# A graph network kernel: four of every 32 gathered edge columns fetched by one-hot products, and node products scaled out of PSUM

## The chip, the cores and the metric

The kernel runs on one core of one Trainium2 chip. The metric is the device time of one execution in microseconds (us). The core has five engines: TensorE (PE, with its weight loads shown apart as PEld), VectorE (DVE), ScalarE (ACT), GpSimd (POOL) and SyncE (SP, which issues plain DMAs). They meet through semaphores.

## The reference

Four layers run over one graph with 6250 nodes, 64 features and 200000 edges sorted by destination. Each layer reads a table of node rows by the source of every edge and sums per destination. The first layer does that three times.

```python
for i in range(3):                                   # layer 0, weights W, b
    mv = proj(mobius_matvec(W[i], h, c), c)
    h = proj(mobius_add(mv, proj(expmap0(b[i][None, :], c), c), c), c)
    ht = logmap0(h, c)
    msgs = edge_weight[:, None] * ht[edge_col]       # a row of the table per edge
    agg = jax.ops.segment_sum(msgs, edge_row, num_segments=N_NODES)
    h = proj(expmap0(jax.nn.relu(logmap0(proj(expmap0(agg, c), c), c)), c), c)
...
h = jnp.maximum(_layernorm(x, axis=-1), 0.0)         # ahead of layers 1, 2 and 3
x = x + _L1_gnn_ref(h, edge_attr_16, ...)            # attention
x = x + _L2_gnn_ref(h, edge_index, edge_attr_8, ...) # relu of [x[src], x[dst], attr] @ W1 + b1, then @ W2 + b2
x = x + _L3_gnn_ref(h, src, dst, ...)                # attention
```

## The kernel before

**Preparation.** In the first 2.1 ms the edges are put into buckets by destination tile. There are T = 49 tiles of 128 nodes. Each bucket is padded to groups of 256 edges, and the groups lie in DRAM as `packed`. There are NG = 832 groups. A group is two columns of 128 edges, one edge a partition.

**Six passes.** PLAN lists three convolution passes ("gcn"), an attention pass, an "mlp" pass and an attention pass. Each pass runs over all 832 groups in ITER = 52 iterations of BODY = 16 groups, that is 32 columns. Before each pass, node work on DVE, PE and ACT makes the table Y (128 partitions x 52 rows x 65 values). SP stores it to DRAM as `table`. Node (tile t, partition p) is row p*52 + t of the table.

**An iteration of a convolution pass.** SP loads 32 columns of row numbers from `SRC` into `idx`, in two halves. POOL issues one indirect DMA for each column (`gathers`, L412), which fetches 128 rows of the table into `G`. `G` has 32 columns, so POOL may refill a column once PE has summed that column's group of the iteration before (`agg_ready`). DVE makes two weighted one-hot matrices for each group (`weighted_one_hot`, L676): 1 times the edge's weight where the destination fits. PE multiplies them with the gathered rows (`sums`, L1346), two f32 products of 128x64 that the trace shows as four passes. DVE adds the result from PSUM to the accumulator of the group's tile (`add_up`, L797). The order on DVE is written out: one-hot of group g, then `add_up` of group g-1. One-hots have a ring of 8 groups. `ps_a` has two banks, so the sums of g wait for `add_up` of g-2.

**Start of an iteration on DVE.** `tiles_of` (L659) loads 24 numbers into registers, which say to which tile each group belongs. In the first convolution pass, `unpack` stands ahead of that for all but the last three iterations. It takes 32 columns out of `packed` for an iteration that comes three later (16 DVE instructions and two that end them).

**Node products.** `node_product` goes through the 52 tiles in 13 steps of 4. PE transposes U, ACT copies the transpose to SBUF, PE multiplies it with weights, and ACT copies the result out of PSUM (`copied`). Ahead of attention, DVE then multiplies Y and er by the reciprocal deviation `small["a"]`. Ahead of the mlp pass, U is scaled and put through a ReLU before the product starts.

## Time and profile before

| what | us |
|---|---|
| median of three runs | 15381.07 |
| lowest and highest of them | 15380.45 to 15383.63 |
| the profiled execution, as timed | 15402.48 |
| its span, first to last instruction | 15400.7 |
| preparation, up to the first gathers | about 2140 |
| convolution passes with their node work | about 2140 to 8660 |
| attention, mlp, attention | about 8660 to 15400 |

The profile divides the span by engine and by line. A row of the timeline has a start, a duration, an engine, a line, the operation, what is written and read, and in brackets how long the engine had been idle and what ended the idle time.

### The profile page before, as it was taken

The numbers are of one execution on the slowest core, as the hardware profiler recorded it, in microseconds if no ns is written. First come the engines' busy times: TensorE is split into PE (matmuls) and PEld (weight loads), VectorE is DVE, ScalarE is ACT, GpSimd is POOL, SyncE is SP. The second block draws the span as 40 slices with busy tenths as digits, with TensorE's granted clock in tenths as the row PEclk, the third lists the DMA queues.
The fourth block names the chain that finished last, engine by engine and source line by source line (L and its number), as shares of the span: only waits on it lengthen the run. The fifth ranks groups of instructions, "written<-read, shape, count | busy, mean of one in ns | idle before, by whom it ended". The sixth has DMA issues, their size and how long they took to land.

```text
span 15400.7 us, 287262 instructions
## 1 busy us (share of the span) xinstructions
PE 7779.5 (51%) x57314; PEld 6635.2 (43%) x57315; DVE 8734.1 (57%) x40002; ACT 3613.7 (23%) x12048; POOL 11064.0 (72%) x11556
## 2 busy tenths in 40 slices
PE   0000004444444444444444588888556565788887
PEld 0000003333333333333333577777444444677777
DVE  7860014444443333433333688888777777788888
ACT  1000000000000000000000366666322222566666
POOL 4777777777767777677777677777577777677776
PEclk9985555555555555555555555555555555555555
DMA  2111112222111111111111111111111111111111
GB/s 97 25 25 26 26 36 41 41 39 41 37 28 27 27 27 27 28 27 27 27 27 27 27 26 26 26 26 26 23 28 28 28 28 28 27 28 27 27 27 28
DMA packets 519941, 468.03 MB, mean 30 GB/s; under 512 B 301517, under 2 KB 326733, under 8 KB 518222
## 3 DMA queue, kind: packets, MB, share of 16 engines
q0 software_dynamic: 369664, 358.70, 14.1%
q1 hardware_dynamic: 149454, 102.38, 2.4%
q14 instruction: 797, 6.53, 0.1%
q8 instruction: 26, 0.43, 0.0%
HBM read 389.15 MB, written 65.20 MB: 30 GB/s over the span
## 4 chain that ended last, share of the span: by engine, by line
DVE 31%; issue 24%; PE 20%; POOL 12%; DVEq 7%; DMA 5%; ACT 1%; POOLq 0%; SPq 0%; ACTq 0%
PE bank L1346 17%; POOL packed L393 9%; DVE OH L676 7%; DMA G<-table,idx 5%; DVE r_gm L709 3%; POOL G L412 3%; DVEq L659 2%; DVE OHB L687 2%; DVE ACC L797 2%; DVE ACC L803 1%; DVE e_arg L754 1%; DVE r_a L712 1%; DVE e_w L749 1%; DVE r_a L716 1%; DVEq L797 1%
## 5 line engine op out<-in xcount | busy, mean ns | idle before, releaser
L412 POOL DMA_INDIRECT G<-table,idx x9984 | 9535.3, 955 | 3614.3 <-issue 2125.6
L1346 PE MATMUL bank<-G,OH 128*128 128x64 f32 x9984 | 2704.1, 428 | 4840.5 <-DVE OH L676 3941.4
L1346 PEld LDWEIGHTS bank<-G,OH 128*128 128x128 f32 x9984 | 2310.9, 322 | 5233.7 <-DVE OH L676 4254.6
L797 DVE TENSOR_TENSOR ACC<-ACC,bank 128x64 f32 x2496 | 552.0, 221 | 3404.0 <-PE bank L1346 3401.8
L393 POOL DMA_INDIRECT packed<-Y,slab_pos x1568 | 1528.5, 975 | 670.3 <-issue 494.7
L676 DVE TENSOR_SCALAR OH<-const,DL,W 128x128 f32<-128x128 f32 x4992 | 1755.8, 400 | 409.2 <-PE bank L1346 269.9
L1346 PE MATMUL bank<-ZR,OH 128*128 128x65 f32 x6656 | 1765.3, 419 | 0.0
L1346 PEld LDWEIGHTS bank<-ZR,OH 128*128 128x128 f32 x6656 | 1623.8, 334 | 0.2
L1408 PE MATMUL bank<-ER,OHT 128*128 x9984 | 995.6, 174 | 712.5 <-DVE negm_lo L738 542.1
L1180 ACT ACTIVATE OHT<-bank 128x256 f32<-128x256 f32 x91 | 35.6, 391 | 5473.0 <-PE bank L1324 5471.9
L1408 PEld LDWEIGHTS bank<-ER,OHT 128*128 128x128 bf16 x9984 | 781.9, 104 | 1005.8 <-issue 877.7
L1396 PE MATMUL bank<-const,V 128*128 128x128 f32 x3328 | 1114.9, 439 | 22.8 <-ACT V L1241 22.6
L687 DVE TENSOR_TENSOR OHB<-iota_b,DLw 128x256 bf16<-128x256 bf16 x2496 | 1054.2, 422 | 38.7 <-ACT V L1241 31.6
L1385 PE MATMUL bank<-ident_b,OHB 128*128 128x128 bf16 x4992 | 1009.1, 305 | 48.8 <-DVE OHB L687 48.8
L1216 ACT ACTIVATE OHT<-bank,const 128x256 bf16<-128x256 f32 x1664 | 788.0, 474 | 527.3 <-PE bank L1385 490.7
L1234 ACT ACTIVATE OH<-OHB,const 128x256 f32<-128x256 bf16 x1664 | 824.9, 496 | 40.5 <-DVE OHB L687 23.3
L1216 ACT ACTIVATE OHT<-bank 128x256 bf16<-128x256 f32 x832 | 319.5, 384 | 1660.1 <-PE bank L1438 1660.1
L709 DVE TENSOR_REDUCE r_gm<-bank 128x1 f32<-128x256 f32 x1664 | 694.3, 417 | 10.5 <-PE bank L1396 10.5
L467 DVE TENSOR_SCALAR W<-Z 128x16 f32 (+1 forms) x104 | 20.4, 196 | 1190.8 <-DMA Z<-packed 1154.9
L1385 PEld LDWEIGHTS bank<-ident_b,OHB 128*128 128x128 bf16 x4992 | 615.9, 135 | 157.9 <-DVE OHB L687 49.8
L1444 PE MATMUL bank<-WE,E8T 128*128 128x128 bf16 x832 | 239.2, 287 | 829.5 <-DVE OH L769 683.4
L1241 ACT ACTIVATE V<-OHB,EL 128x128 f32<-128x128 bf16 x1664 | 576.7, 393 | 227.7 <-DVE EL L695 211.0
(273 smaller groups left out, 14164.1 us busy)
## 6 DMA issues: line engine op xcount, KB each, us to landing
G<-table,idx POOLq DMA_INDIRECT x9984
packed<-Y SPq DMA_DIRECT2D x42, 640.0 KB, 17.7
Z<-packed SPq DMA_DIRECT2D x104, 256.0 KB, 2.7
Y<-in_payload SPq DMA_DIRECT2D x98, 256.0 KB
packed<-Y,slab_pos POOLq DMA_INDIRECT x1568
table<-Y SPq DMA_DIRECT2D x6, 1690.0 KB, 5.5
idx<-SRC SPq DMA_DIRECT2D x624, 8.0 KB
X<-in_x SPq DMA_DIRECT2D x1, 1568.0 KB, 8.3
```

The lines of the kernel that those rows point to most:

```text
L393: pool.indirect_dma_start(out=packed_rows, out_offset=bass.IndirectOffsetOnAxis(ap=slab_pos[:, h, c:c + 1], axis=0), in_=slab[:, h, c, :], ...
L412: pool.indirect_dma_start(out=G[:, 2 * q + c, :], out_offset=None, in_=table, in_offset=bass.IndirectOffsetOnAxis(ap=idx[:, h, j:j + 1], a ...
L676: o = v.tensor_scalar(OH[:, q, c, :], iota, DL[:, at], W[:, at], ALU.is_equal, ALU.mult)
L687: v.tensor_tensor(OHB[:, q, :, :], iota_b[:, :].unsqueeze(1).to_broadcast([P, 2, P]), DLw[:, 2 * u:2 * u + 2].unsqueeze(2).to_broadcast([P ...
L709: v.tensor_reduce(sr["gm"][:, r:r + 1], ps_x[r % 2][:, 0:GE], AX.X, ALU.max).then_inc(a_done, 1)
L797: v.tensor_tensor(acc, acc, ps_a[r % 2][:, 0:D], ALU.add).then_inc(acc_done, 1)
L1216: return a.activation(OHT[:, r, :], ps_m[r % 2][:, 0:GE], ACT.Identity, scale=scale, bias=bias)
L1234: a.activation(OH[:, q, :, :], OHB[:, q, :, :], ACT.Identity, scale=-1.0, bias=ones[:, 0:1])
L1346: o = pe.matmul(ps_a[r % 2][:, 0:w], OH[:, q, c, :], parts[c], start=c == 0, stop=c == 1)
L1385: o = pe.matmul(ps_m[r % 2][:, c * P:(c + 1) * P], OHB[:, q, c, :], ident_b[:, :], start=True, stop=True)
L1396: o = pe.transpose(ps_x[r % 2][:, c * P:(c + 1) * P], V[:, r % 4, c, :], ident)
L1408: pe.matmul(e[:, c:c + 1], one, ER3[:, bass.ds(t, 1), k], start=k == 0, stop=k == 2)
```

## The change

**Four columns from a table on chip.** In a convolution pass POOL gathers only the first 28 of 32 columns of each iteration (`fetched(n)` is 14 groups of 16). Groups 14 and 15 get their rows otherwise. Before the pass, `three_parts` splits the table Y into three bf16 parts that add up to it (`table_parts`, 49 tiles x 3 x 64, in the memory of U and Z). In an iteration, DVE copies the four columns of row numbers (`choose`, at group 10 of the iteration before). PE spreads them over all partitions with four f32 products against the identity (`spread`, at group 12). ACT subtracts 52 times the partition number while it copies to bf16 (`codes`). At the start of the iteration DVE compares this 128x512 code with each tile number 0 to 48, one instruction a tile (`tile_hots`). PE multiplies each result's four 128x128 matrices with the 128x192 table parts of that tile (`rows_from_table`), and sums over the tiles in two banks. At group 4 DVE adds the three parts out of PSUM into `G` (`take_rows`). The compared matrices have 8 slots, so DVE is at most 8 tiles ahead of PE.

**Node products.** In products 3 to 6 DVE, not ACT, takes the result out of PSUM and multiplies by `small["a"]` or adds on the way (`each_step`). ACT puts the ReLU on the transposes. The whole-table multiplications and the ReLU on DVE go. The product starts as soon as U is centred, ahead of the squares. DVE's part of the eviction comes after its reduction and the square root.

```diff
@@ gathers, indices: fetched(n) of 16 groups
+        def fetched(n):
+            return BODY - ON_CHIP // 2 if PLAN[n][0] == GCN else BODY
-                        for q in range(BODY // 2 * h, BODY // 2 * (h + 1)):
+                        for q in range(BODY // 2 * h, min(BODY // 2 * (h + 1), fetched(n))):
@@ DVE
+                def choose(i):
+                    need(v, code_spread, i + n * (ITER + 1))
+                    at = i * (2 * BODY) + (2 * BODY - ON_CHIP)
+                    move(chosen[:, :], SRC[:, ds(at, ON_CHIP)]).then_inc(chosen_ready, 1)
+                def tile_hots(i):
+                    j = i * T + n * ITER * T
+                    v.wait_ge(code_ready, i + (n * (ITER + 1) + 1))
+                    for tile in range(T):
+                        need(v, tile_used, j + max(tile - SLOTS + 1, 0))
+                        v.tensor_scalar(tile_hot(tile), code, float(tile), None, ALU.is_equal).then_inc(tile_ready, 1)
+                def take_rows(i):
+                    v.wait_ge(tile_used, i * T + (n * ITER * T + T))
+                    need(v, agg_ready, i * BODY + gb)
+                    for k in range(ON_CHIP // 2):
+                        q = BODY - ON_CHIP // 2 + k
+                        got = ps_rows[k][:, 0:6 * D].rearrange("p (s k c) -> p s c k", s=2, k=3)
+                        v.tensor_reduce(G[:, 2 * q:2 * q + 2, 0:D], got, AX.X, ALU.add).then_inc(taken[k], 1)
...
+                    if live(0) and u == 0:
+                        tile_hots(i)
+                    if live(0) and u == 4:
+                        take_rows(i)
+                    if live(0) and u == 10:
+                        choose(i + 1)
@@ PE
+                def spread(i):
+                    pe.wait_ge(chosen_ready, i + (n * (ITER + 1) + 1))
+                    need(pe, code_ready, i + n * (ITER + 1))
+                    for c in range(ON_CHIP):
+                        o = pe.matmul(ps_code[:, c * P:(c + 1) * P], chosen[:, c:c + 1].to_broadcast([P, P]), ident,
+                                      start=True, stop=True)
+                    o.then_inc(code_spread, 1)
+                def rows_from_table(i):
+                    for k in range(ON_CHIP // 2):
+                        need(pe, taken[k], i + n * ITER)
+                    for tile in range(T):
+                        pe.wait_ge(tile_ready, i * T + (n * ITER * T + tile + 1))
+                        for c in range(ON_CHIP):
+                            o = pe.matmul(ps_rows[c // 2][:, c % 2 * 3 * D:(c % 2 + 1) * 3 * D],
+                                          tile_hot(tile)[:, c * P:(c + 1) * P],
+                                          table_parts[:, tile, :, :].rearrange("p k c -> p (k c)"),
+                                          start=tile == 0 and c % 2 == 0, stop=tile == T - 1 and c % 2 == 1)
+                        o.then_inc(tile_used, 1)
...
+                        if u == 0:
+                            rows_from_table(i)
+                        if u == 12:
+                            spread(i + 1)
@@ before each convolution pass
+                three_parts([table_parts[:, :, k, :] for k in range(3)], Y[:, :, 0:D], sums_of)
@@ node products, attention
+                def take(at, got):
+                    own.count(v.tensor_tensor(small["er"][:, at], got[:, :, ROW], small["a"][:, at], ALU.mult))
+                    return scaled(Y[:, at, :], got[:, :, 0:ROW], at)
                 centre_and_start()
-                tt(Y[:, :, :], Y[:, :, :], small["a"][:, :].unsqueeze(2).to_broadcast([P, TP, ROW]), ALU.mult)
-                tt(nodes(small["er"]), nodes(small["er"]), nodes(small["a"]), ALU.mult)
+                each_step(take)
```

The order of instructions on DVE, at the start of an iteration of the first convolution pass, was this before (OH are the one-hots of a group, ACC the accumulator, sched the tile numbers):

```order
L1036 SCALAR_TENSOR_TENSOR SRC<-itmp 128x16
L659 ISA
L659 TENSOR_LOAD sched
L661 ISA x2
L80 REGISTER_ALU
L676 ISA
L676 TENSOR_SCALAR OH<-const,DL,W 128x128
L676 ISA
L676 TENSOR_SCALAR OH<-const,DL,W 128x128
```

In the changed kernel the same place on DVE begins so (OHT and V hold the compared matrices, OHB the code), and 46 more such comparisons follow:

```order
L1120 SCALAR_TENSOR_TENSOR SRC<-itmp 128x16
L703 ISA
L703 TENSOR_LOAD sched
L705 ISA x2
L755 REGISTER_ALU
L83 REGISTER_ALU
L758 TENSOR_SCALAR OHT<-OHB 128x512
L758 TENSOR_SCALAR V<-OHB 128x512
L758 TENSOR_SCALAR OHT<-OHB 128x512
```

The 49 comparisons stand between the register load and the first one-hots of the iteration, so also ahead of the last `add_up` of the iteration before.

On PE, an iteration began before with a wait and the sums of one group after another:

```order
L276 UNCONDITIONAL_BRANCH
L276 ISA
L1350 ISA
L80 REGISTER_ALU
L1346 MATMUL bank5<-G,OH 128x64 x2
L1356 REGISTER_ALU
L1346 MATMUL bank6<-G,OH 128x64 x2
```

Now 49 such blocks of four products stand ahead of the first sums (UZ holds the table parts; three of the blocks are shown):

```order
L1456 REGISTER_ALU
L1458 MATMUL bank2<-UZ,OHT 128x192 x2
L1458 MATMUL bank3<-UZ,OHT 128x192 x2
L1456 REGISTER_ALU
L1458 MATMUL bank2<-UZ,V 128x192 x2
L1458 MATMUL bank3<-UZ,V 128x192 x2
L1456 REGISTER_ALU
L1458 MATMUL bank2<-UZ,OHT 128x192 x2
L1458 MATMUL bank3<-UZ,OHT 128x192 x2
```

No sums of the iteration can start before the last of these 196 products has been issued.

## Rows read from the trace of the kernel before

**Rows 1.** The page: busy time by engine, and the granted TensorE clock in 40 slices.
```profile
PE 7779.5 (51%) x57314; PEld 6635.2 (43%) x57315; DVE 8734.1 (57%) x40002; ACT 3613.7 (23%) x12048; POOL 11064.0 (72%) x11556
...
PEclk9985555555555555555555555555555555555555
```

**Rows 2.** Groups by line in the second convolution pass, 4372 to 6452 us.
```profile
L412 POOL DMA_INDIRECT G<-table,idx x1663 | 1573.5, 946 | 562.3 <-issue 290.9 <-PE bank L1346 215.8 <-DMA idx<-SRC 55.5
L1346 PE MATMUL bank<-G,OH 128*128 128x64 f32 x3320 | 903.9, 428 | 1213.3 <-DVE OH L676 946.4 <-DMA G<-table,idx 144.4 <-issue 117.1
```

**Rows 3.** Timeline, DVE between two iterations: first pass (2628), second pass (5293).
```profile
2628.51 0.22 DVE L797 TENSOR_TENSOR ACC<-ACC,bank 128x64 f32 x1 [1.54 <-PE bank L1346]
...
2635.81 0.60 DVE L676 TENSOR_SCALAR OH<-const,DL,W 128x128 f32<-128x128 f32 x2 [2.25 <-issue]
...
5293.57 0.22 DVE L797 TENSOR_TENSOR ACC<-ACC,bank 128x64 f32 x1 [1.62 <-PE bank L1346]
5296.37 0.64 DVE L676 TENSOR_SCALAR OH<-const,DL,W 128x128 f32<-128x128 f32 x2 [2.58 <-PE bank L1346]
```

**Rows 4.** Timeline after an unpack, when gathered rows lie ready and DVE and PE catch up.
```profile
2636.68 1.96 PE L1346 MATMUL bank<-G,OH 128*128 128x64 f32 x8 [5.83 <-DVE ACC L797]
...
2637.94 0.22 DVE L797 TENSOR_TENSOR ACC<-ACC,bank 128x64 f32 x1 [0.88 <-PE bank L1346]
...
2638.80 0.22 DVE L797 TENSOR_TENSOR ACC<-ACC,bank 128x64 f32 x1
...
2640.16 0.22 DVE L797 TENSOR_TENSOR ACC<-ACC,bank 128x64 f32 x1 [0.50 <-PE bank L1346]
...
2641.16 0.22 DVE L797 TENSOR_TENSOR ACC<-ACC,bank 128x64 f32 x1
```

**Rows 5.** Timeline in the mlp pass: a bf16 instruction on DVE, six bf16 products on PE.
```profile
11503.18 0.19 DVE L467 TENSOR_SCALAR E8S<-V 128x128 bf16<-128x128 bf16 x1
...
11503.28 0.30 DVE L777 SCALAR_TENSOR_TENSOR OH<-OH 128x128 f32<-128x128 f32 x1
...
11503.60 0.50 PE L1458 MATMUL bank<-OH,OHB 128*128 128x65 bf16 x6
```

**Rows 6.** Timeline, PE in a node product: its first passes, and passes 5 us later.
```profile
4320.32 2.08 PE L1324 MATMUL bank<-const,ACC 128*128 128x128 f32 x8 [0.62 <-DVE n_res L644]
...
4325.46 0.61 PE L1324 MATMUL bank<-const,ACC 128*128 128x128 f32 x4
```

**Rows 7.** Stretches: length, busy time (instructions) of PE, PEld, DVE, ACT, POOL, PE clock, DMA.
```profile
4324.40:4334.00 9.60, 9.42 (x84) 9.22 (x83) 9.53 (x3) 9.38 (x42) 0.00 (x0) 1.00 0.00 1
4335.00:4338.00 3.00, 0.00 (x0) 0.00 (x0) 2.50 (x1) 1.69 (x4) 0.00 (x0) 1.00 0.00 0
...
11028.50:11031.70 3.20, 2.38 (x32) 1.76 (x32) 3.13 (x16) 1.11 (x5) 2.29 (x4) 0.97 0.14 23
11032.00:11038.00 6.00, 5.54 (x64) 4.19 (x63) 5.86 (x32) 2.00 (x9) 4.47 (x6) 0.50 0.18 28
```

**Rows 8.** Timeline in the preparation: an indirect DMA issued beside a long DVE instruction.
```profile
978.44 3.62 DVE L451 TENSOR_TENSOR U<-X,n_a 128x3328 f32<-128x3328 f32 x1
979.03 3.87 POOL L393 DMA_INDIRECT packed<-Y,slab_pos  x1 [0.30 <-issue]
```

**Rows 9.** Groups by line and shape, whole span: DVE reduces 256 values out of PSUM.
```profile
L709 DVE TENSOR_REDUCE r_gm<-bank 128x1 f32<-128x256 f32 x1664 | 694.3, 417 | 10.5 <-PE bank L1396 10.5
```

**Rows 10.** Timeline, DVE: the last node product, and a split of a node tensor into bf16 parts.
```profile
13165.51 3.62 DVE L451 TENSOR_TENSOR Z<-U 128x3328 f32<-128x3328 f32 x1
...
13171.10 0.15 DVE L644 COPY n_res<-n_r 128x1 f32<-128x1 f32 x1
...
13185.90 3.68 DVE L451 TENSOR_TENSOR Y<-Y,n_a 128x3380 f32<-128x3380 f32 x1 [9.15 <-ACT Y L1204]
...
11003.75 1.90 DVE L1093 CAST U<-Z 128x3328 bf16<-128x3328 f32 x1
11005.68 3.62 DVE L451 TENSOR_TENSOR Z<-Z,U 128x3328 f32<-128x3328 f32 x1
```

More of the change, by code:

```diff
@@ L51 @@
 AHEAD = 3
+ON_CHIP = 4
+SLOTS = 8
 STEPS_N = TP // 4
@@ L483, in _ @@
             own.count(v.memset(sched[:, :], 0))
+            own.count(v.memset(SRC[:, 2 * NG:], 0))
             own.count(v.memset(rank, 0.0))
@@ L926, in run_pass, with three_parts @@
                 own.wait()
+            def three_parts(parts, what, rest):
+                own.wait()
+                own.count(v.tensor_copy(parts[0], what))
+                tt(rest, what, parts[0], ALU.subtract)
+                own.wait()
+                own.count(v.tensor_copy(parts[1], rest))
+                tt(parts[2], rest, parts[1], ALU.subtract)
             v.wait_ge(sched_loaded, 16)
```

126 lines of the change are left out of this document (82 added, 44 removed).

## The prediction

> **What bounds the kernel now.** I read the page first: POOL is busy 72% of the span, more than any other engine, and the TensorE clock stands at 0.5, that is 1.2 GHz, from the fourth slice on [rows 1]. Then the groups by line in the second convolution pass: 1663 gathers fill 1573.5 + 562.3 us, so one starts every 1.28 us with the pass's start in it, and PE is idle for more time than it is busy [rows 2]. Inside an iteration the step is steadier: 0.95 us and a gap of 0.30, 1.25 us, so 32 columns take 40.1 us. Over 52 iterations that is 2085 us, which is the length of the pass. A convolution pass is bound by POOL's gathers; DVE and PE wait for them. The question is what PE and DVE need for an iteration once they have more to do.
>
> **What is removed.** Four gathers of 1.25 us in each of 156 iterations: 5.0 us an iteration, 780 us in all, if nothing else then needs more than 35.1 us.
>
> **What is added on the path of DVE and PE.** The stretch stands in one piece at the start of an iteration, and the work around it is serial: DVE cannot begin it before `add_up` of group 14, and PE cannot sum group 0 before it is over. So I add up one turn, from `add_up` of group 14 to the next one.
>
> - Start of the iteration on DVE: from one `add_up` to the next instruction 5296.37 - 5293.57 = 2.8 us [rows 3], the register load. POOL covered it before; nothing covers it now, since PE has only group 15 left. The first comparison and its hand-over to PE: 0.5 us, estimated from the 0.3 us that an instruction of that size should take (next but one).
> - The 196 products on PE. Six bf16 products of 64 or 65 columns take 0.50 us [rows 5]; the last one's 0.24 off, that is a step of 0.053 us for 64 columns at 1.2 GHz, with the weight loads hidden. For 192 columns: 0.159 us, 31.2 us for 196. The clock decides. In a node product PE worked without a pause from 4320.32, the f32 steps were 0.213 us (eight passes in 2.08, the first of them a little longer), and from 4324.4 the clock is 1.00 (2.4 GHz) and four passes take 0.61 us, a step of 0.111 [rows 6, 7]: half, and 5 ns. The stretch is denser than that product, so I take the same 4.1 us at 1.2 GHz (26 products), and 170 at 0.083 us: 18.2 us.
> - The 49 comparisons on DVE run beside it. A bf16 instruction of 128 values takes 0.19 us and the next starts 0.10 us after it [rows 5]. 384 more values at four a cycle of 0.96 GHz are 0.10 us: one each 0.20 us, 9.8 us, behind PE's 0.33 us a tile. Covered. At one value a cycle it would be 0.60 us each and 29.4 us, the bound then.
> - The sums of groups 0 to 14. Four passes end 1.1 us after their start (eight take 1.96) [rows 4]. After that DVE and PE go hand in hand, as where they catch up: `add_up` at 2637.94, 2638.80, 2640.16, 2641.16, so two groups in 2.22 and 2.36 us, 2.29 in the mean [rows 4]. 1.1 + 7 x 2.29 = 17.1 us.
> - `take_rows` at group 4: two reductions of 384 values; 256 take 0.417 us [rows 9], so 0.55 each and about 0.5 from start to start: 1.0 us on DVE's path.
> - `spread` at group 12: four f32 products of 128 columns, eight passes of 0.213 us, 1.7 us, less the 0.2 us for which PE pauses at each group there: 1.5 us. ACT's copy and `choose` (0.1 us) are done while groups 13 to 15 are summed.
> - A credit: the clock stays up some 3.5 us after dense work (still 1.00 up to 4338 though PE is not busy from 4335; at 11028.5, with PE busy for 74% of the time, it held for 3.2 us and was 0.50 after that) [rows 7]. Passes at 0.111 take 0.41 us less for a group, and their drain 0.15 less, so 0.56 us for each pair, of which one group's passes lie on the turn. Two pairs: -1.1 us.
> - Hand-over to `add_up`: 0.2 us.
>
> The sum is 2.8 + 0.5 + 18.2 + 17.1 + 1.0 + 1.5 - 1.1 + 0.2 = 40.2 us, against 40.1 before. POOL's 35.1 us lie below it, so they go off the path: the 5 us that the gathers lose are handed to PE and DVE nearly to the last tenth. For 156 iterations: +0.14 x 156 = +22 us.
>
> **The first pass pays more.** There DVE also unpacks: from `add_up` to the next one-hot 2635.81 - 2628.51 = 7.3 us [rows 3], 4.5 more than elsewhere. Before, POOL went on gathering meanwhile and the catching up was free. Now it lies on the turn, 49 times: +220 us.
>
> **Node work.** `three_parts` ahead of each convolution pass: 1.9 + 3.6 + 1.9 + 3.6 = 11 us [rows 10]. Part of it lies beside the table's store, the index load and the first gather's landing, which DVE waited for before; I take 5 us each, +15 (bounds 0 and 33). For attention, 24.1 us went from the centred U to the end of the product with 3.7 us of scaling (13165.5 to 13189.6) [rows 10]. Now the product starts 5.6 us earlier, stops after two steps until DVE has reduced (about 10 us later), and then needs 11 steps at 1.7 us cold or 0.9 warm, some 12.5 us: 2 us less, twice. Product 4 loses a scaling of 3.6 us and a ReLU of 1.9, and squares and reduction (3.6 each) now lie beside it; of these 12.7 us I count all. Product 5 overlaps two of its three whole-table instructions, 7 us. Together -24 us (bounds -40 and +10).
>
> **Sum.** +22 + 220 + 15 - 24 = +233 us on the profiled execution's own 15402.5: 15635. That execution is 21.4 us above the median, so the forecast for a median is 15614; call it 15610.
>
> **Bounds.** The unknowns are the clock and how tightly DVE and PE go hand in hand. Low end: PE stays at 2.4 GHz all through. Then a group's passes end in 0.65 us, a pair takes 0.56 less, 1.73, and spreading 0.8: 2.8 + 0.5 + 18.2 + 0.65 + 12.1 + 1.0 + 0.8 + 0.2 = 36.3 us. High end: the rise comes at 6 us instead of 4.1 (+1.0), and waits on 49 semaphores cost PE 0.03 each (+1.2): 42.4.
> The Trainium skill ("TensorE: Matmul & The Clock Gate", "Back-to-back issue gap") gives a real stream of load and product pairs 81 ns at 128 columns and 131 at 512, warm, so about 90 ns at 192 by interpolation, an estimate from that page; the stretch would be 1.2 us longer by it, and the forecast some 190 us higher. The rows have no warm bf16 stream to hold against it; the cold one steps at exactly its columns.
>
> **Rivals.**
> - Faster: the turn is shorter than I add up. The break-even is 156 x (turn - 40.06) + 220 + 15 - 24 = 0, a turn of 38.7 us. For it: the clock holds in the sums, or DVE, which has finished its last comparisons while PE still has eight tiles to go, gains more than I gave. Against: at 11031.7 the clock fell after 74% busy [rows 7], and at 2.4 GHz a group's passes would fill at most 0.6 of 0.87 us, 70%. At the low end, 36.3 us: 104 x -3.8 + 49 x 0.7 - 3 x 3.8 - 9 = -381 us, 15000. Milder: a turn of 38, 15270.
> - The clock does not rise in the stretch: 31.2 us for it and no credit, a turn of 54.3 us, +2430 us, 17810. Against: it rose within 4.1 us in the node product, and the mlp pass with its bf16 products reached 0.97 too [rows 6, 7].
> - The comparison runs at one value a cycle: 29.4 us, a turn of 51.4, +1980 us, 17360.
> - The comparisons keep POOL out. An indirect DMA that began beside a 3.6 us DVE instruction took 3.87 us instead of 0.96 [rows 8], so POOL waits for such an instruction to end. If it only waits for one or two comparisons a gather, 0.4 us on some 11 gathers, POOL needs 39.5 us, still under the turn, and nothing changes. If it finds no gap in 9.8 us of comparisons it needs 45, and the time is +750 us, 16130. The Trainium skill ("SBUF — State Buffer", "Who interferes with whom") calls this an exclusive lock on a port pair that VectorE and GpSimd share, taken by VectorE instructions in a two-port mode, as these comparisons would be; by that rule, the trace agrees that POOL can be held.
>
> **How the numbers follow.** 0.2% is 31 us, about what a measurement of this kernel can tell from no change. Forecast, turns of 38.9 to 42.4 us: 0.52. A turn under 38.5: 0.27, of which 0.06 below 15060. The strip between: 0.06. POOL kept out: 0.06. Clock stays down: 0.05. Comparisons slow: 0.04. So faster 0.27, same 0.06, slower 0.67. The range 15060 to 15930 leaves out the last three and the fastest 0.05. The forecast case's own range is 15410 to 15930.
>
> **What would show it.** In the changed profile, second pass: first sums of iterations 40.2 us apart; POOL idle between gathers, released by PE's sums; the 196 products in about 18 us, their steps 0.16 and then 0.083 us, the granted clock 1.00 in two thirds of the stretch and 0.50 in the rest of the turn; one comparison each 0.33 us, waiting for PE; the first pass 4.5 us an iteration longer. Wrong if POOL's gathers still stand 1.25 us apart without breaks, or if the clock stays at 1.00 while groups are summed.

## The result, and the profile after

The changed kernel takes **15487.7 us** (median, 15481.8 to 15491.1) where the kernel before takes 15380.8: a ratio of 1.0069, 95% interval 1.0057 to 1.0081. It is 107 us slower; the forecast was 229 us slower. A second set of runs gave 15492.2 against 15384.1, again 1.0069. The direction holds, the size of the loss was put twice too high, and part of the loss has another cause than the forecast named (below). The profiled execution has a span of 15485.7 us, 85 us over that of before (15400.7), and the accounts below are made on the spans.

The page, busy time by engine and the clock's row, to hold against [rows 1]:

```profile
PE 10353.6 (67%) x89162; PEld 9340.3 (60%) x89163; DVE 10816.0 (70%) x48212; ACT 3695.3 (24%) x12116; POOL 10590.1 (68%) x10932
...
PEclk9985556666677777777777655555555555555555
```

POOL has 624 instructions fewer and is no longer the busiest engine by far. TensorE and VectorE stand level with it, and the clock's row has risen from 5 to 6 and 7 in the convolutions alone.

The groups by line in the second convolution pass, 4578 to 6590 us (busy time, mean ns of one, idle time ahead of them and what ended it), to hold against [rows 2]:

```profile
L440 POOL DMA_INDIRECT G<-table,idx x1451 | 1411.2, 973 | 582.5 <-issue 370.2 <-PE bank L1434 212.3
L1434 PE MATMUL bank<-G,OH 128*128 128x64 f32 x3321 | 705.0, 377 | 154.9 <-DVE OH L720 139.7 <-DVE ACC L864 3.8
L1458 PE MATMUL bank<-UZ,OHT 128*128 128x192 bf16 x5200 | 704.2, 263 | 129.2 <-DVE OHT L758 129.2
```

POOL's 1411 + 582 us still fill the pass, but the idle part is no longer its own pace alone: 0.40 us a gather instead of 0.34, and about once a turn POOL waits for TensorE, up to 4 us (below). TensorE's wait for one-hots went from 946 us to 140, and it waits another 129 us for comparisons.

One turn, that is the work of TensorE and VectorE for one iteration, as the timeline has it in the third pass. Lines between the ones shown are left out. First the end of the stretch of table products (L1458), the sums (L1434) with their `add_up` (L864), and `take_rows` (L767):

```profile
7599.29 0.49 PE L1458 MATMUL bank<-UZ,V 128*128 128x192 bf16 x4
7599.49 0.29 DVE L758 TENSOR_SCALAR OHT<-OHB 128x512 bf16<-128x512 bf16 x1
...
7601.23 1.02 POOL L440 DMA_INDIRECT G<-table,idx  x1 [0.30 <-issue]
7602.55 1.01 POOL L440 DMA_INDIRECT G<-table,idx  x1 [0.30 <-issue]
...
7605.89 1.03 PE L1434 MATMUL bank<-G,OH 128*128 128x64 f32 x8
7606.62 0.22 DVE L864 TENSOR_TENSOR ACC<-ACC,bank 128x64 f32 x1 [1.60 <-PE bank L1434]
...
7607.27 1.02 POOL L440 DMA_INDIRECT G<-table,idx  x1 [3.71 <-PE bank L1434]
...
7608.52 1.02 DVE L767 TENSOR_REDUCE G<-bank 128x128 f32<-128x384 f32 x2
...
7613.02 0.22 DVE L864 TENSOR_TENSOR ACC<-ACC,bank 128x64 f32 x1 [0.68 <-PE bank L1434]
...
7615.13 0.22 DVE L864 TENSOR_TENSOR ACC<-ACC,bank 128x64 f32 x1 [0.46 <-PE bank L1434]
```

Then its other end: the last `add_up`, the register load, and the next stretch, first at half clock and then at full:

```profile
7623.15 0.22 DVE L864 TENSOR_TENSOR ACC<-ACC,bank 128x64 f32 x1 [0.68 <-PE bank L1434]
...
7625.93 0.29 DVE L758 TENSOR_SCALAR OHT<-OHB 128x512 bf16<-128x512 bf16 x1 [2.56 <-issue]
...
7626.28 0.82 PE L1458 MATMUL bank<-UZ,OHT 128*128 128x192 bf16 x4 [2.43 <-DVE OHT L758]
...
7631.37 0.85 PE L1458 MATMUL bank<-UZ,OHT 128*128 128x192 bf16 x4
7632.01 0.62 PE L1458 MATMUL bank<-UZ,V 128*128 128x192 bf16 x4
7632.47 0.49 PE L1458 MATMUL bank<-UZ,OHT 128*128 128x192 bf16 x4
7632.80 0.49 PE L1458 MATMUL bank<-UZ,V 128*128 128x192 bf16 x4
```

And the granted clock behind the stretch (columns as in [rows 7]):

```profile
7606.00:7611.40 5.40, 3.53 (x25) 2.86 (x23) 4.52 (x17) 0.00 (x0) 3.22 (x4) 1.00 0.09 14
7612.00:7630.00 18.00, 14.74 (x72) 13.84 (x73) 10.19 (x41) 0.69 (x1) 13.43 (x16) 0.50 0.16 26
```

All that the prediction named is there: TensorE waits for VectorE's first comparison through 2.43 us, four products step by 0.64 us and then by 0.33, a comparison comes each 0.33 us, and POOL stands still for 3.71 us until TensorE has summed group 0.

Where the 85 us lie. A pass is counted from its first register load to its 53rd (52 iterations); the gaps are what lies between the passes. All in us:

| | before | after | difference | forecast |
|---|---|---|---|---|
| first convolution | 2088.8 | 2278.4 | +189.6 | |
| second | 2084.8 | 2015.0 | -69.8 | |
| third | 2085.0 | 2015.5 | -69.5 | |
| convolutions together | 6258.6 | 6308.9 | +50 | +242 |
| start and gaps | 2625.3 | 2629.9 | +5 | -9 |
| fourth, fifth, sixth pass, code unchanged | 6516.8 | 6546.9 | +30 | 0 |

### The profile page after: what moved, and what is told of

Read it like the earlier page. It is cut to its first block, busy times and chain, and to the rows that moved or that the text cites. A ratio compares the mean times of both kernels' runs of the same rounds, so it can differ in the third digit from the quotient of the medians.

```text
span 15485.7 us, 373775 instructions
## 1 busy us (share of the span) xinstructions
PE 10353.6 (67%) x89162; PEld 9340.3 (60%) x89163; DVE 10816.0 (70%) x48212; ACT 3695.3 (24%) x12116; POOL 10590.1 (68%) x10932
## 4 chain that ended last, share of the span: by engine, by line
PE 36%; DVE 23%; issue 16%; POOL 11%; DVEq 8%; DMA 4%; ACT 1%; POOLq 0%; ACTq 0%; SPq 0%
PE bank L1458 19%; PE bank L1434 10%; POOL packed L421 9%; DMA G<-table,idx 4%; DVEq L703 3%; DVE OH L720 3%; POOL G L440 3%; DVE r_gm L776 2%; PE bank L1516 2%; PE bank L1447 2%; PE bank L1528 2%; DVE OHB L731 2%; DVE ACC L870 1%; DVE e_arg L821 1%; DVE ACC L864 1%
## 5 line engine op out<-in xcount | busy, mean ns | idle before, releaser
L440 POOL DMA_INDIRECT G<-table,idx x9360 | 9064.0, 968 | 4173.8 <-issue 2263.8
L1458 PE MATMUL bank<-UZ,OHT 128*128 128x192 bf16 x15600 | 2135.2, 265 | 598.8 <-DVE OHT L758 598.8
L1434 PE MATMUL bank<-G,OH 128*128 128x64 f32 x9984 | 2151.7, 381 | 451.2 <-DVE OH L720 396.9
L1434 PEld LDWEIGHTS bank<-G,OH 128*128 128x128 f32 x9984 | 1943.7, 285 | 645.1 <-DVE OH L720 575.3
L1458 PE MATMUL bank<-UZ,V 128*128 128x192 bf16 x14976 | 2026.1, 262 | 0.0
L1458 PEld LDWEIGHTS bank<-UZ,OHT 128*128 128x128 bf16 x15600 | 1480.8, 105 | 649.8 <-DVE OHT L758 619.3
L1434 PE MATMUL bank<-ZR,OH 128*128 128x65 f32 x6656 | 1765.2, 419 | 0.0
L1434 PEld LDWEIGHTS bank<-ZR,OH 128*128 128x128 f32 x6656 | 1623.7, 334 | 0.2
L758 DVE TENSOR_SCALAR OHT<-OHB 128x512 bf16<-128x512 bf16 x3900 | 1179.8, 303 | 608.3 <-issue 380.7
L1458 PEld LDWEIGHTS bank<-UZ,V 128*128 128x128 bf16 x14976 | 1430.6, 105 | 22.0
L758 DVE TENSOR_SCALAR V<-OHB 128x512 bf16<-128x512 bf16 x3744 | 1111.3, 297 | 198.7 <-PE bank L1458 104.8
L864 DVE TENSOR_TENSOR ACC<-ACC,bank 128x64 f32 x2496 | 548.5, 220 | 992.9 <-PE bank L1434 937.1
L1447 PE MATMUL bank<-const,chosen 128*128 128x128 f32 x1272 | 321.5, 434 | 1295.8 <-DVE chosen L495 1295.8
```

Source lines behind the costliest of these rows:

```text
L440: pool.indirect_dma_start(out=G[:, 2 * q + c, :], out_offset=None, in_=table, in_offset=bass.IndirectOffsetOnAxis(ap=idx[:, h, j:j + 1], a ...
L758: v.tensor_scalar(tile_hot(tile), code, float(tile), None, ALU.is_equal).then_inc(tile_ready, 1)
L864: v.tensor_tensor(acc, acc, ps_a[r % 2][:, 0:D], ALU.add).then_inc(acc_done, 1)
L1434: o = pe.matmul(ps_a[r % 2][:, 0:w], OH[:, q, c, :], parts[c], start=c == 0, stop=c == 1)
L1447: o = pe.matmul(ps_code[:, c * P:(c + 1) * P], chosen[:, c:c + 1].to_broadcast([P, P]), ident, start=True, stop=True)
L1458: o = pe.matmul(ps_rows[c // 2][:, c % 2 * 3 * D:(c % 2 + 1) * 3 * D], tile_hot(tile)[:, c * P:(c + 1) * P], table_parts[:, tile, :, :].re ...
```

## The experiments

Two chips that some runs fell on took some 20000 us for the kernel before instead of 15384. Their runs stand last.

**The comparisons ahead of the register load** (`load_late_third`, 15139.5 us, ratio 0.9828, interval 0.9811 to 0.9844). Three lines: `tile_hots` moves from the first step of an iteration to the place ahead of `tiles_of`, which loads the row numbers.

```diff
                     if u is None:
                         windows(i)
+                        if kind == GCN:
+                            tile_hots(i)
                         t = tiles_of(i, tregs)
...
-                    if live(0) and u == 0:
-                        tile_hots(i)
```

> The changed kernel with the 49 comparisons ahead of the loading of the row positions. Theory A (TensorE stands still for the loading in the changed kernel): the turn of the second and third pass takes 36.3 to 36.7 us instead of 38.75, the first pass 41.3 to 42.0 instead of 43.8, ratio 0.983 to 0.985. Theory B (part of what unpack_between gained in the first pass was the comparisons' place): first pass 40.0 to 40.5, ratio 0.978 to 0.980.

Theory A held in its mechanism, a little short in size: from `add_up` of group 14 to the next one a turn of the second and third pass takes 36.8 us in the mean instead of 38.75, so 1.95 us less and not 2.3. (The passes can't be compared by their register loads here, since the load itself has moved behind the stretch; by that count the turn would be 36.5.) The first product comes 2.2 us earlier and the stretch is 0.65 us shorter, but the sums behind it take 0.9 us more, since the load now holds up VectorE there. In the first pass a turn takes 40.8 us instead of 43.9, between the two theories: the stretch loses 1.1 us there, because the clock rises about 3 us into it and no longer 5.8. The rows of the second pass (VectorE's first one-hot behind the load, TensorE's first sums):

```profile
5539.81 0.60 DVE L720 TENSOR_SCALAR OH<-const,DL,W 128x128 f32<-128x128 f32 x2 [2.15 <-issue]
...
5540.63 1.43 PE L1436 MATMUL bank<-G,OH 128*128 128x64 f32 x8 [0.67 <-DVE ACC L864]
```

VectorE still stands still for the load, but TensorE, which was up to 8 tiles of 0.33 us behind it, waits for only 0.67 us at the head of its sums, where it waited 2.43 at the head of the stretch. So of the 2.8 us that the prediction put at the head of the sum about 2 were on the path because of their place.

**The unpacking between the comparisons** (`unpack_between`, 14914.5 us, ratio 0.9693, interval 0.9677 to 0.9709). The edit above, and in the first pass one of the unpacking's instructions behind each comparison from the ninth on:

```diff
+                        if tile >= SLOTS:
+                            next(between, None)
...
-                    unpack(i + AHEAD)
-                    body(None, i)
+                    body(None, i, unpacking(i + AHEAD))
```

> Two edits of the changed kernel: the 49 comparisons stand behind VectorE's loading of the row positions instead of ahead of it, and in the first convolution the 18 small instructions that unpack the next iteration's edges stand between the comparisons instead of ahead of them. In the changed kernel the first table product of a first-pass turn starts 7.6 us behind the sum of group 14, in the other passes 3.15, and VectorE is paced by TensorE during the stretch. Theory A (the 4.5 us of unpacking is the first pass's own loss and the stretch has room for it on VectorE, whose comparison takes 0.29 of 0.33 us): each pair of comparisons gains no room, since 0.29 + 0.04 fill the step; 18 instructions of 0.06 to 0.2 us make the stretch longer by what they take, so the first pass gains only the semaphore waits between them, 1 to 2 us a turn, 50 to 100 us in all. Theory B (the stretch is bound by TensorE, 0.083 us a product, and VectorE can run ahead by 8 slots): 4.5 us x 48 turns = 216 us gained, which brings the kernel to 0.993 of the kernel before.

(That text has the first edit the wrong way round: the comparisons stand ahead of the loading here, as in the diff.) Theory B held, and the whole ratio is lower than its 0.993, since that counted the unpacking alone. Against the kernel of the last experiment the first pass falls by another 211 us, from 2102.6 to 1891.4, and its turn is as long as that of the other passes, 36.7 us from `add_up` to `add_up`. Theory A erred in counting a comparison at its recorded 0.29 us; its successor can start 0.20 us after it (rows of `one_part` below; 0.22 in the mean), so each 0.33 us has some 0.11 to spare. The cost of unpacking that the prediction laid on the path, 220 us, was there, and the stretch had room for it.

**The stretch in pieces** (`spread_out`, 14825.0 us, ratio 0.9636, interval 0.9620 to 0.9652).

```diff
-                    for tile in range(T):
+                    for tile in range(4 * u, min(4 * u + 4, T)):
...
-                        if u == 0:
-                            rows_from_table(i)
+                        if u < 13:
+                            rows_from_table(i, u)
```

Four comparisons stand ahead of each of the first 12 one-hots on VectorE, and 16 products ahead of each of the first 12 sums on TensorE, with the last comparison and its four products at the thirteenth; `take_rows` and `spread` come at group 13.

> The changed kernel with its 49 comparisons and 196 table products spread over the 13 first groups of an iteration, 4 comparisons and 16 products ahead of each group's sum, instead of one stretch ahead of the first. Theory A (the stretch pays because it lifts TensorE's clock to 2.4 GHz for some 14 of its 18 us): in pieces of 16 products the clock stays at 1.2 GHz for most of the turn, a product takes 0.16 us instead of 0.083, 196 x 0.077 = 15 us more a turn, 156 turns: +2300 us, near 17800, ratio 1.15. Theory B (TensorE is busy enough through the whole turn for the clock to stay up): products stay at 0.083 to 0.1 us, the float32 sums get quicker as well, and each group's sum waits less for its one-hot; the turn falls to 34 to 37 us, ratio 0.97 to 0.99.

Theory B held, and the ratio is a little below its 0.97: the clock did not fall, it rose. A window in the second pass, and the second pass's gathers by line:

```profile
4800.00:5200.00 400.00, 328.83 (x3015) 309.35 (x3012) 269.26 (x1123) 7.56 (x11) 304.30 (x315) 0.85 0.17 27
```

```profile
L440 POOL DMA_INDIRECT G<-table,idx x1451 | 1407.9, 970 | 442.2 <-issue 391.6 <-PE bank L1434 50.6
```

The clock is 0.85 in the mean, where the changed kernel has 0.75 from 5200 to 5600 us, with the same work. POOL's gathers fill 1408 + 442 us, 1.275 each, and no break of several microseconds is left: the turn is 35.7 us in all three passes, 0.6 over the 28 x 1.25 = 35.1 that the gathers need. The pass is bound by POOL again, and the four gathers taken away give 4.4 of their 5.0 us a turn.

**One part of the table** (`one_part`, 14758.1 us, ratio 0.9593, interval 0.9577 to 0.9609): 64 columns a product instead of 192. This kernel leaves out two of the table's three parts, and `take_rows` has a third of the values to add.

```diff
-                                          table_parts[:, tile, :, :].rearrange("p k c -> p (k c)"),
+                                          table_parts[:, tile, 0, :],
```

> The changed kernel with one of the table's three bf16 parts alone: each table product has 64 columns instead of 192, and the rows taken from PSUM are the sum over one part. The other two parts are left out. Theory A (TensorE's columns set the stretch while its clock is up: 192 / 2.4 GHz = 0.080 us of the measured 0.083): with 64 columns VectorE's comparisons set it, 49 x 0.29 = 14.2 us instead of 18.0, less 0.5 for the shorter reduces: about 4 us a turn x 156 = -650 us, ratio 0.965. If the clock no longer rises since TensorE has a third of the columns, the float32 sums behind the stretch lose what they gained (some 1.2 us a turn) and the gain is 2.8 us a turn, ratio 0.98. Theory B (the stretch is bound by what a product costs whatever its columns, weights and issue): 18 us stay and the ratio stays at 1.005 to 1.009.

Theory A had the cause right, columns, and the size of the stretch wrong. It takes 10.7 us, not 18.0 and not 14.2. The comparisons set it now, and most come 0.20 us apart:

```profile
4871.19 1.04 POOL L440 DMA_INDIRECT G<-table,idx  x1 [0.30 <-issue]
4871.33 0.29 DVE L758 TENSOR_SCALAR V<-OHB 128x512 bf16<-128x512 bf16 x1
...
4871.53 0.29 DVE L758 TENSOR_SCALAR OHT<-OHB 128x512 bf16<-128x512 bf16 x1
...
4871.73 0.29 DVE L758 TENSOR_SCALAR V<-OHB 128x512 bf16<-128x512 bf16 x1
...
4871.94 0.41 DVE L758 TENSOR_SCALAR OHT<-OHB 128x512 bf16<-128x512 bf16 x1
...
4872.27 0.27 DVE L758 TENSOR_SCALAR V<-OHB 128x512 bf16<-128x512 bf16 x1
```

This is the prediction's 0.20 us. But one comparison in six is recorded with 0.41 us and its successor starts 0.33 us after it, some 8 times in a stretch. Such a comparison starts 0.74 us (median) after the start of a gather, as in the rows shown, so the gather is the likely cause. The mean is 0.22, and 49 take 10.7 us and not 9.8. The turn falls by 3.0 us and not by 7 in the second and third pass, since POOL's 35.7 us end it; in the first it falls by 8.1.

**The node part alone** (`node_third`, 15388.5 us, ratio 0.9994, interval 0.9984 to 1.0003): `fetched(n)`, the comparisons and the table products left as they were before, products 3 to 6 as in the change.

> The node part of the change alone, convolutions as before. Theory A: 15345 to 15375 us where the kernel before takes 15384, ratio 0.997 to 1.000, and the two gaps ahead of the second and third convolution stay at 52 us, since on the slower chips they were 52.6 and 52.8 us without the table and 63 with it; the gaps ahead of the fourth and fifth pass shrink by 7 and 10 us. Theory B: what the slower chips showed (0.992) holds everywhere, 15260.

Theory A: 10 us under the kernel before, which took 15398.9 in this set of runs. The gaps ahead of the second and third convolution are 52.6 and 52.0 us (52.3 and 52.1 before), so the 10.4 and 11.1 us that the changed kernel has more there are the table's split. The gaps ahead of the fourth, fifth and sixth pass shrink by 4.8, 8.6 and 9.3 us, 22.7 in all. The three passes themselves move by +16.9, +8.3 and -17.1 us, though their loops are the same.

**VectorE's code at another place** (`shifted_again`, 15541.0 us, ratio 1.0092, interval 1.0075 to 1.0109; `spread_shifted`, 14688.5 us, ratio 0.9538, interval 0.9522 to 0.9553). The first is the changed kernel, the second the one with the stretch in pieces (`if n == 5`, `range(8)`):

```diff
+                if n == 3:
+                    for _ in range(24):
+                        own.wait()
+                        own.count(v.memset(small_ring["negm"][:, :], START))
                 clear_sums()
```

> The changed kernel with 24 such memsets ahead of the fourth pass. On a chip where TensorE's ends come late the pause of 0.37 us had moved within the turn, and the time could not be read. Theory A (VectorE's pauses are set by where the loop lies): the fourth pass goes from 2280 us to 2248 to 2262 or above 2290. Theory B: it stays at 2278 to 2283.

> The kernel with the table products spread over 13 groups, and 8 small VectorE memsets, each behind a wait on the last, ahead of the sixth pass. That pass took 2276 us there instead of 2162 to 2172, and in its trace VectorE stands still for 2.2 us a turn between two instructions of its loop's head, 0.1 us in the other kernels. Theory A (the head lies across an edge of what VectorE fetches of its program at once, and the memsets move it off): the sixth pass takes 2165 to 2180 us and the total falls by 95 to 110 us, to 14715 to 14730, ratio 0.957. Theory B (the pause comes from elsewhere): the sixth pass stays at 2270 to 2280.

Theory A in both, though the sixth pass fell further than its 2165 to 2180 us. The fourth pass, with its loop unchanged, went from 2279.9 to 2344.8 us, the sixth from 2275.8 to 2131.3. What changes can be read off VectorE's timeline. A place in the fourth pass, before and after the change:

```profile
9530.48 0.28 DVE L803 SCALAR_TENSOR_TENSOR ACC<-ACC,r_corr,bank 128x65 f32 x1
9530.68 0.15 DVE L754 TENSOR_TENSOR e_arg<-e_w,bank 128x2 f32<-128x2 f32 x1
```

```profile
9615.58 0.28 DVE L870 SCALAR_TENSOR_TENSOR ACC<-ACC,r_corr,bank 128x65 f32 x1
9616.14 0.16 DVE L821 TENSOR_TENSOR e_arg<-e_w,bank 128x2 f32<-128x2 f32 x1 [0.28 <-issue]
```

0.20 us from start to start before and 0.56 now, with nothing to wait for ("issue"), at the same place in every turn. Compared instruction by instruction in the mean of 48 turns, the changed kernel has new pauses of 0.37, 0.35 and 0.15 us, lacks one of 0.12, and has one of 0.32 at another place. The turn is 0.62 us longer, which is the 32 us that this pass lost in 52 turns. With the 24 memsets these new pauses are gone, two others of 0.36 have come, and the loop's head takes 1.8 us more: 1.25 us a turn in all, the 65 us. The head of the sixth pass's loop in `spread_out`, then in `spread_shifted`:

```profile
13417.37 0.16 DVE L783 SCALAR_TENSOR_TENSOR r_a<-r_a 128x1 f32<-128x1 f32 x1
13422.67 0.18 DVE L495 TENSOR_SCALAR DLw<-DL 128x32 f32 x1 [5.14 <-issue]
```

```profile
13301.53 0.16 DVE L783 SCALAR_TENSOR_TENSOR r_a<-r_a 128x1 f32<-128x1 f32 x1
13304.61 0.18 DVE L495 TENSOR_SCALAR DLw<-DL 128x32 f32 x1 [2.92 <-issue]
```

Eight instructions of filler took 2.2 us a turn away, 52 x 2.2 = 114 of the 144 us. The rest lies inside the turn, where three pauses of 0.36 us are gone and one is new. The time at which the pass starts is not the cause: in `one_part`, whose VectorE executes exactly as many instructions ahead of the fourth pass as in the changed kernel, the pass starts 737 us earlier, takes 2280.9 us and has the pauses at the same places. That the pauses are fetches of code is an inference: the runs show that they follow the place of the code, no more.

**The changed kernel again** (`after_again`, 15492.2 us, ratio 1.0069, interval 1.0052 to 1.0086).

> The changed kernel once more, beside the runs that follow, since the last group of runs met a chip on which the kernel before took 20005 us instead of 15381. There the durations of single instructions were the same, but the semaphore of a float32 node or edge product arrived some 2 us (mean 2.3) after the modelled end, 0.02 before. Theory A (the late ends belong to that chip or hour, not to the kernels): on an undisturbed chip the ratio is 1.007 again, within 1.005 to 1.009, and the turn of the second pass takes 38.7 us. Theory B (the change costs what it costs on any chip by the work that TensorE does): the ratio is 1.10 wherever the kernel before takes 20000 us, and 1.007 where it takes 15400.

It was run since the first experiments had fallen on a slower chip. This one fell on an undisturbed chip, so it shows only that the ratio repeats there, which both theories say. On a slower chip the changed kernel ran with filler only (1.1210, below).

**On the two slower chips** (the kernel before 20004.7 us on one, 19950.5 on the other), first the four runs that were meant to split the change. `node_only` and `conv_only` each undo one half of it (the convolutions, or products 3 to 6, as in the kernel before), `load_late` is the edit of `load_late_third`, and `two_columns` is one line:

```diff
-ON_CHIP = 4
+ON_CHIP = 2
```

> The kernel before with the change's node products alone (products 3 to 6 taken out of PSUM and scaled by DVE); all 32 columns of a convolution are gathered. My theory, from the gaps between passes in the changed kernel: about 24 us less than before, 15357 us, with every pass as long as before. Rival: the attention pass after it becomes longer (the changed kernel's first attention pass took 32 us more than before's), then about 15390 us.

> The changed kernel with the node products of before: the four columns from the table on chip alone. My theory: the turn of DVE and PE is 38.7 us in the second and third convolution pass and 44.2 in the first, as in the changed kernel, so about 24 us more than the changed kernel, 15511 us. Rival: the two parts meet somewhere, and the sum of their effects is not the effect of both (off by over 15 us).

> The changed kernel with 2 columns of 32 from the table on chip, not 4: 30 gathers, 98 products in the stretch, 49 comparisons of 256 values. My theory: the stretch takes 4.1 + 72 x 0.083 = 10 us, the turn of DVE and PE about 30.5 us (35 in the first pass), so POOL's 30 x 1.252 = 37.6 us bind in all three passes: 156 x -2.5 us against before, -390, and some -5 from the rest: 14985 us. Rival: the comparisons hold POOL's gathers back through a shared port, or the work added costs in any case: then gathers are longer than 1.25 us in the stretch and the time is 15200 us or more.

> The changed kernel with the register load of tile numbers on DVE put behind the 49 comparisons, not ahead of them. DVE ends the comparisons some 2.4 us before PE ends the products, so the load hides there. My theory (a serial turn of DVE and PE binds all 156 iterations): each turn is 2.2 to 2.4 us shorter, 36.4 us in the second pass, 350 us in all, 15135 us. Rival (POOL or the port binds in part): under 100 us gained.

| | one chip | the other chip | undisturbed |
|---|---|---|---|
| node part alone | 0.9917 | 0.9924 | 0.9994 |
| convolutions alone | 1.1115 | 1.1136 | |
| two columns on chip instead of four | 1.0534 | | |
| comparisons ahead of the load | 1.0981 | 1.0994 | 0.9828 |
| filler ahead of the fourth pass | | 1.1210 | 1.0092 |

The second column is from the same kernels, run once more:

> The node part of the change alone, the convolutions as before (28 by 8 columns all gathered). It was run on the chip where the kernel before took 20005 us and was 0.9917 of it. Theory A (the sum of the prediction: the scaled evictions leave PSUM with VectorE and save 24 us in all, 15 us come back in the gaps, so 10 to 40 us are gained): 15345 to 15375, ratio 0.997 to 1.000. Theory B (the gaps of the changed kernel, 10.5 and 11.1 us longer ahead of the second and third convolution, are the node part's, not the table's): 10 to 25 us lost, ratio 1.001 to 1.002.

> The changed kernel with one edit: the 49 comparisons of an iteration stand ahead of the loading of its row positions and of the first one-hot, instead of behind them; unpacking stays where it was. Theory A (in the changed kernel TensorE stands still for the 2.8 us of loading, since its stretch of table products can't start; in the other order the loading lies beside the last products): the turn of the second and third pass takes 36.3 to 36.7 us instead of 38.75, as in the run in which the unpacking was moved too, the first pass 41.3 to 42.0 instead of 43.8; 2.3 x 156 = 360 us gained, ratio 0.983 to 0.985. Theory B (half of what that run gained in the first pass belonged to the comparisons' place, since 7.4 us is more than unpacking's 4.5 and loading's 2.3): first pass 40.0 to 40.5, ratio 0.978 to 0.980.

> The convolutions of the changed kernel with the node products of the kernel before. Theory A (the two parts do not touch each other): the ratio is that of the changed kernel less that of the node part alone, 1.007 to 1.010, and not the 1.11 it had on the chip where the kernel before took 20005 us. Theory B (the table products, which every pass reads from SBUF, also slow the node part): ratio 1.004 or below.

> The changed kernel with 24 small VectorE memsets, each behind a wait on the last, ahead of the fourth pass, so that VectorE's code from there on lies elsewhere in its program; the loops themselves are the same. They take some 4 us once. Theory A (the fourth pass took 2280 us instead of 2248 because VectorE's instructions pause for 0.37 us once or twice a turn at places set by where the loop lies): the fourth pass goes to another of these levels, 2248 to 2260 or above 2290, and the last two passes move by up to 20 us a pass. Theory B (the 32 us come from something that the convolutions leave behind, such as the tables on chip or the clock): the fourth pass stays at 2278 to 2283 us and the total grows by 4 us.

None of these ratios says what the change does on an undisturbed chip, and all verdicts above rest on the other runs. The convolutions alone and the kernel with two columns were never measured on an undisturbed chip. So the convolutions' own cost is known only as a difference, and whether two columns would have been faster is open. What is different there shows in one and the same kernel (the node part alone), second convolution pass, on a slower chip and then on an undisturbed one:

```profile
L1361 PE MATMUL bank<-G,OH 128*128 128x64 f32 x3324 | 857.7, 430 | 1633.0 <-DVE OH L691 929.1 <-issue 587.1 <-DVE ACC L812 101.0
...
L812 DVE TENSOR_TENSOR ACC<-ACC,bank 128x64 f32 x830 | 182.9, 220 | 1649.2 <-remote 1190.8 <-PE bank L1361 268.9 <-issue 182.2
```

```profile
L1361 PE MATMUL bank<-G,OH 128*128 128x64 f32 x3324 | 905.6, 428 | 1214.4 <-DVE OH L691 944.8 <-DMA G<-table,idx 150.1 <-issue 119.6
...
L812 DVE TENSOR_TENSOR ACC<-ACC,bank 128x64 f32 x831 | 183.5, 221 | 1203.2 <-PE bank L1361 1203.2
```

VectorE's instruction takes as long as elsewhere (220 against 221 ns). TensorE's is recorded with 430 against 428 ns, but the ends of its products are modelled in this profile, so that says little. `add_up` waits for something that the profile can't name ("remote") for 1191 us of 2456. One such wait, in the convolutions alone on that chip:

```profile
7622.56 1.12 PE L1434 MATMUL bank<-G,OH 128*128 128x64 f32 x4 [4.62 <-issue]
...
7630.15 0.22 DVE L864 TENSOR_TENSOR ACC<-ACC,bank 128x64 f32 x1 [7.64 <-remote]
```

The sums end at 7623.7 by the profile, and `add_up` starts 6.5 us later. The turn in the second pass was 47.4 us without table products, 54.3 with two columns' and 61.5 with four columns', so some 7 us more for 98 products, which is no more than their own 8 us at 0.083 us. The lost time lies in the sums: in the convolutions alone the first product comes after 3.13 us and the stretch takes 18.5 (18.0 elsewhere), but from the last table product to `add_up` of group 14 it is 39 us instead of 17.5, and 38.6 with two columns. Why is not known; both chips did it in every run.

## Why the prediction was right in direction and twice too high

**What bounds the pass: right.** The gathers left the path, and what replaced them is a turn of VectorE and TensorE. POOL waits (3.71 us behind each stretch).

**Start of the iteration, 3.3 us: right.** From `add_up` to the first product it is 3.15 us in the mean; 3.13 in the rows (7623.15 to 7626.28). Moving the load off the path showed it from the other side.

**The stretch, 18.2 us: right.** 18.0 in the mean of the second and third pass, with a warm step of 0.0826 us for 192 columns (7599.29 and the products behind it step by 0.33 for four) and the rise after 4.0 us in the mean (4.1 was taken). The mean hides three kinds of turn, with the rise 5.7, 3.5 and 2.8 us into the stretch and turns of 40.0, 38.1 and 37.9 us. The Trainium skill ("TensorE: Matmul & The Clock Gate", "Back-to-back issue gap") gave some 90 ns by interpolation; the measured 82.6 are lower, and the prediction was right to leave those 1.2 us out of the sum. The formula that the same section keeps for a single product without its load, columns at 2.4 GHz and 2.5 ns, gives 82.5 and would have been the better guide.

**The sums and what stands among them, 18.7 us: this is the term that was mis-sized.** It was 17.1 + 1.0 + 1.5 - 1.1 + 0.2; measured, from the last table product's start to `add_up` of group 14, 17.5 us in the second and third pass. In the means over the second pass, group 0 is added 0.8 us behind the stretch, where the prediction had 1.1 + 0.2: it is summed at full clock, for which no credit was given. From there to group 14 it is 16.7 us against 17.4. The two pairs with credit take 1.74 and 1.73 us, as forecast. The other five, less 1.5 for spreading, take 2.08, 2.14, 2.33, 1.92 and 2.28, in the mean 2.15 and not 2.29. The first of them has the clock for a part: behind the stretch it stays at 1.00 for 5.6 us in two of the three kinds of turn (7606.00 to 7611.40 is one of them) and for 3.8 in the third, 5.0 in the mean and not 3.5. The 2.29 was the mean of two pairs behind an unpack [rows 4] and was 0.14 us too long as a model of the rest; 7613.02 to 7615.13 is 2.11.

Together 1.2 us here and 0.3 in the two terms ahead: a turn of 38.75 us instead of 40.2. Times 156 that is -225 us, the whole of the miss and more. The prediction had written down its break-even, 38.7, and the measured turn lies on it, in the strip between 38.5 and 38.9 to which it gave 0.06. With this turn its own sum gives +7 us, that is no change. So the direction came out right in good part by luck: what made the kernel slower are the two next terms, both put too low, and one that wasn't in the sum.

**The first pass, +220 us: a little too low.** The turn is 43.8 us there, 5.1 over the others in the mean of 52, so 263 us. 4.2 of it is the start (7.57 us to the first product in the turns that unpack), 0.7 the stretch, where the clock rises after 5.8 us instead of 4.0, and 0.3 lies in the sums behind it.

**Node work, +15 and -24: the second right in its sum, the first too low.** The gaps in which the node products lie shrink by 23.5 us in the changed kernel and by 22.7 with the node part alone. The sum is right because its parts cancel: by the node part alone 4.8 us came where 2 were forecast (ahead of the first attention), 8.6 for 12.7 (ahead of the mlp pass) and 9.3 for 9 (ahead of the second attention). Splitting the table costs 6.4 ahead of the first convolution, 10.4 and 11.1 ahead of the others, 28 in all and within the bounds (0 to 33): ahead of the second and third nearly nothing of the 11 us was hidden.

**Nothing for the passes whose code is the same: wrong by 30 us.** They moved by +32.1, +8.2 and -10.2 us, and the experiments with filler show that the place of VectorE's loop in its program is enough for that. In the fourth pass the pauses account for all of it; in the other two this is likely and was not traced.

The account closes: +242 for the convolutions became +50 (-225 for the turn, +43 for the first pass, -9 because the three passes of before took 6258.6 us and not the 6249 of 156 turns at 40.06), -9 became +5, and 0 became +30: +85 on the spans for +233.

**The rivals.** The clock rose, so 17810 fell. A comparison took 0.20 us where it ran free (0.22 in the mean), so 17360 fell. POOL was hardly held by the comparisons: a gather beside them takes 1.02 us instead of 0.94, with the same 0.30 behind it (7601.23, 7602.55), 1.32 apart instead of 1.25. The Trainium skill ("SBUF — State Buffer", "Who interferes with whom") calls the port pair's use an exclusive lock; by these rows it costs a gather 0.07 us beside instructions of 0.29 us, and one comparison a gather comes 0.13 us late (`one_part`), and only the 3.6 us instruction of [rows 8] held one for long. That was an instruction with two input tensors, of another kind than the comparisons.

**What the prediction did not see** is that the turn was not a property of the change but of its order. The load ahead of the comparisons (1.95 us a turn), the unpacking ahead of them (4.1 us a turn in the first pass) and the one stretch (another 1.1 us, down to POOL's limit) were each taken as given. The kernel with the stretch in pieces and 8 instructions of filler takes 14688.5 us, 4.6% less than the kernel before and 5.3% less than the changed one, with the same gathers and the same table.

## What to carry to other kernels

Work that is moved off a full engine onto two half-idle ones buys nothing while those two work by turns: write down one turn, and then ask of each term (a register load, an unpacking, a block of products) whether it could stand beside another instead of ahead of it. Cut a new block of work into the pieces of the loop that it joins, rather than put it at its head. And where a forecast stands within a microsecond or two a turn of its break-even, its sign hangs on pairs measured elsewhere: say so, and take the steps from a stretch with the same neighbours.

## What the runs showed of the hardware that was not expected

- VectorE's loop runs at a speed that depends on where its code lies in its program. 8 or 24 small instructions ahead of a pass moved its time by -144 and +65 us of some 2200, by pauses of 0.36 us inside the turn and 1.8 to 2.2 us at the loop's head. On the whole kernel that is 0.2 to 0.9%, as much as the change itself, and the time of the passes that nobody touched shows it.
- GpSimd's gathers and VectorE's bf16 comparisons seem to slow each other, by little: beside comparisons a gather takes 1.02 us instead of 0.94, and one comparison a gather takes 0.41 us instead of 0.29.
- TensorE's clock stays up for longer behind dense bf16 products than was read off the kernel before: 5.6 us in most turns and 3.8 in the rest, with TensorE busy for 3.53 of 5.40 us in the turn shown. In pieces of 16 products between sums it stood at 0.85 in the mean over 400 us, higher than with all 196 in one stretch (0.75).
- The rise into the stretch came 2.8, 3.5 or 5.7 us after its start, in an order that repeats over the turns.
- On two of the chips the end of TensorE's sums reached VectorE late, by 6.5 us in the rows shown, while VectorE's instructions kept their duration. Whether the sums themselves were late can't be told, since their ends are modelled. The kernel before took 30% longer there, and the change's convolutions cost 11%, where the whole change cost 0.7% elsewhere.
